# Attention and the last stage in one block: the last attention row carries up products of the last stage's first row

## The reference, cut to what matters

```python
xn  = layernorm(x)
s   = attn(xn)                                   # attention block with its own MLP
g   = silu(ffn(xn))                              # mixture of 8 low-rank maps, gated by a softmax
out = x + s * g

def attn(x):                                     # on xn
    a = rmsnorm(x, ln1_w)
    q, k, v = a @ Wq, a @ Wk * 32**-0.5, a @ Wv  # 16 heads, key width 16, value width 32
    gk = log_sigmoid(a @ Wkg1 @ Wkg2 + bkg2) / 16
    S_t = S_(t-1) * exp(gk_t) + k_t v_t^T ;  o_t = q_t S_t        # linear recurrence over tokens
    o = silu(a @ Wg + bg) * normalize_per_head(o)
    x = x + o @ Wo                               # called xmid in the kernel
    b = rmsnorm(x, ln2_w)
    return x + (silu(b @ W1) * (b @ W3)) @ W2    # W1, W3: 512 x 1408, W2: 1408 x 512
```

## Time and profile before

| | |
|---|---|
| time, median of 3 runs | 1734.0 us (1733.23, 1734.0, 1738.09) |
| the profiled execution | 1738.03 us, of which the profile's span is 1736.3 us |
| granted TensorE clock, mean | 0.979 of full speed |
| TensorE busy | 1640.8 us (95%), 12272 matmuls |
| VectorE, ScalarE, POOL busy | 855.2, 566.9, 153.5 us |
| TensorE in the chain that ended last | 43% of the span |
| HBM | 76.89 MB read, 33.57 MB written |

### The profile page before, as it was taken

One profiled execution on the slowest core, in us unless ns is written; L12 is line 12 of the kernel. 1 busy time (PEld: TensorE's weight loads), 2 busy tenths in 40 slices (PEclk: granted clock), 3 DMA queues, 4 the chain that ended last, 5 costly groups with the idle time before them and its releaser, 6 DMA issues. The chain is left out here.

```text
span 1736.3 us, 30613 instructions
## 1 busy us (share of the span) xinstructions
PE 1640.8 (95%) x12272; PEld 1289.1 (74%) x12272; DVE 855.2 (49%) x1334; ACT 566.9 (33%) x959; POOL 153.5 (9%) x183
## 2 busy tenths in 40 slices
PE   6999999869899999999984899999999999999998
PEld 4777777647677777777763678788787878787886
DVE  5555555237767968877863435141422324141413
ACT  3333333225535635635532241211212121212110
POOL 4650000020101101101000000000000000000000
PEclk9999999989999999999997899999999999999999
DMA  7353332010101101201102324002030303030110
GB/s 159 115 123 75 98 84 73 25 61 2 55 24 54 79 0 79 79 0 79 72 2 97 116 85 173 20 26 94 0 121 0 121 0 121 0 121 0 48 50 25
DMA packets 49429, 110.98 MB, mean 64 GB/s; under 512 B 13088, under 2 KB 24432, under 8 KB 41200
## 3 DMA queue, kind: packets, MB, share of 16 engines
q1 hardware_dynamic: 46640, 97.83, 17.8%
q10 hardware_dynamic: 1152, 8.39, 1.2%
q0 software_dynamic: 1600, 4.25, 0.9%
HBM read 76.89 MB, written 33.57 MB: 64 GB/s over the span
## 5 line engine op out<-in xcount | busy, mean ns | idle before, releaser
L1290 DVE TENSOR_TENSOR m_h<-m_ps,m_silu 128x512 f32<-128x512 f32 x88 | 60.9, 692 | 434.3 <-PE m_ps L1437 434.3
L1363 ACT ACTIVATE m_silu<-m_ps 128x512 f32<-128x512 f32 x88 | 52.5, 597 | 298.8 <-PE m_ps L1437 298.0
L1435 PE MATMUL m_ps<-m_xshi,m_w1hi 128*128 128x512 f32 x352 | 143.3, 407 | 6.3 <-DVE m_xslo L1283 6.3
L1435 PE MATMUL m_ps<-m_xshi,m_w3hi 128*128 128x512 f32 x352 | 140.7, 400 | 4.7 <-ACT m_silu L1363 4.7
L1437 PE MATMUL m_ps<-m_xshi,m_w3lo 128*128 128x512 f32 x352 | 140.0, 398 | 0.0
L1436 PE MATMUL m_ps<-m_xslo,m_w3hi 128*128 128x512 f32 x352 | 140.0, 398 | 0.0
L1436 PE MATMUL m_ps<-m_xslo,m_w1hi 128*128 128x512 f32 x352 | 139.8, 397 | 0.0
L1437 PE MATMUL m_ps<-m_xshi,m_w1lo 128*128 128x512 f32 x352 | 139.7, 397 | 0.0
L892 POOL TENSOR_TENSOR row<-row,a_r 128x512 f32<-128x512 f32 x32 | 48.7, 1553 | 635.6 <-DMA a_r<-scratch_r 635.6
L1435 PEld LDWEIGHTS m_ps<-m_xshi,m_w1hi 128*128 128x128 f32 x352 | 66.5, 189 | 25.2 <-issue 9.5
L831 DVE TENSOR_TENSOR a_a<-a_att,causal 128x1024 f32<-128x1024 f32 x64 | 75.5, 1218 | 16.6 <-PE a_att L1035 16.6
(11 more groups left out here) (245 smaller groups left out, 3834.1 us busy)
## 6 DMA issues: line engine op xcount, KB each, us to landing
row<-scratch_xn SPq DMA_DIRECT2D x16, 1024.0 KB, 5.0
row<-scratch_xmid SPq DMA_DIRECT2D x16, 1024.0 KB, 7.0
m_xt<-in_L_attn_W SPq DMA_DIRECT2D x33, 256.0 KB, 3.2
f_xt<-in_L_attn_x SPq DMA_DIRECT2D x32, 256.0 KB, 8.8
scratch_xn<-row SPq DMA_DIRECT2D x8, 1024.0 KB, 9.7
scratch_gate<-row ACTq DMA_DIRECT2D x8, 1024.0 KB, 3.9
scratch_xmid<-row SPq DMA_DIRECT2D x8, 1024.0 KB, 3.9
row<-scratch_gate SPq DMA_DIRECT2D x8, 1024.0 KB, 10.1
```

The costliest lines, as they stand in the source:

```text
L1290: dve.tensor_tensor(h[n], dense.region(f"b{j}"), silu[n], ALU.mult).then_inc(dense.taken_sem(f"b{j}"), 1)
L1363: act.activation(silu[n], dense.region(f"a{j}"), ACT.Silu).then_inc(dense.taken_sem(f"a{j}"), 1)
L1435: pe.matmul(ps, wh, xh, start=k == 0, stop=False)
```

## The change

Five things are changed together.

1. Attention and last stage share one block. `phase_a` no longer opens a block; it hands its engine streams over as functions, and `phase_m` calls them with a class `Front`. What the last attention row passed over is now work of the last stage's row 0: slot k0 makes up a of block 0, k1 up b of block 0, u and q0 up a and b of block 1, q1 and v1 up a and b of block 2, and z down product 0. Where the next row's x was scaled and split, xmid of row 0 is. The weight pieces 0 to 11 are loaded from the moment VectorE has finished the last product with the q tiles, into `xt`, and 0 to 10 are split between the chunks. The weights now lie per block j (`w[j]`).
2. The squares, the sum on POOL, the mean-square matmul and 1/rms for the last stage move into the attention: in row i they are made of the output of row i - 1, one square in chunk 0, and so on, and 1/rms is stored to HBM (`scratch_r2`, 2 KB a row) and loaded, broadcast, beside x. The buffer of the squares is that of `cum`, so the next row's scan waits for the store. The last row's are made in row 0 of the last stage.
3. In the first stage, row 0 is normed in two halves of two token tiles, W1 comes in four pieces, and ScalarE waits for the bias only after it has filled x.
4. At the end of a row the add of xmid and the multiply by the gate alternate block by block.
5. The last row is turned block by block, and stored in four transfers.

```diff
@@ phase_a: squares of the row before, on ScalarE, POOL, TensorE @@
+            def squares(i, ms):
+                for m in ms:
+                    if m > 1:
+                        act.wait_ge(*count.at("x2sum", i, m - 1))
+                    act.activation(added if m else square, xn[:, m, :], ACT.Square).then_inc(count.sem("x2"), 1)
+            def deviation(i):
+                act.wait_ge(*dense.ready("ms", i))
+                act.activation(added[0:1], dense.region("ms")[0:1], ACT.Ln, bias=eps[0:1]).then_inc(dense.taken_sem("ms"), 1)
+                act.wait_ge(*dense.taken("ms", i))
+                act.activation(added[0:1], added[0:1], ACT.Exp, scale=-0.5).then_inc(count.sem("r2"), 1)
...
+                for m in range(1, KT):
+                    pool.wait_ge(*count.at("x2", i, m + 1))
+                    pool.tensor_tensor(square, square, added, ALU.add).then_inc(count.sem("x2sum"), 1)
...
+                    if c + 1 == NC:
+                        pe.wait_ge(*dense.free("ms", i))
+                        pe.wait_ge(*count.at("x2sum", i))
+                        pe.matmul(dense.region("ms"), avg_all, square, start=True, stop=True).then_inc(dense.ready_sem("ms"), 1)
@@ SP in an attention row, and VectorE ahead of the scans @@
+                sp.wait_ge(*count.at("r2", i))
+                sp.dma_start(row(r2_d, i), added[0:1]).then_inc(count.sem("r2_out"), 16)
+                sp.wait_ge(*count.at("x2", i))
                 sp.wait_ge(*count.at_before("xmid_out", i))
...
+                    dve.wait_ge(*count.at_before("r2_out", i))
                     for gc in range(g * NC, (g + 1) * NC):
@@ phase_m: what fills the last attention row @@
+            def sync(sp):
+                sp.wait_ge(*a.count.at("mqh", NB - 1))
+                sp.wait_ge(*a.dense.ready(f"g{LAST}", NB - 1))
+                sp.dma_start(ln2, ...).then_inc(s_ln2, 16)
+                load_weights(sp, 0, 3 * FRONT + 3)
...
+                # VectorE
+                work = {"split": split, "c0": first_hidden, "u": second_a, "c2": lambda: weights_lo(dve, 6, 7),
+                        "c3": lambda: weights_lo(dve, 7, 9), "upper": second_and_third}
...
+                # TensorE
+                work = {"k0": lambda: up("k0", 0, 0), "k1": lambda: up("k1", 0, 1), "u": lambda: up("u", 1, 0),
+                        "q0": lambda: up("q0", 1, 1), "q1": lambda: up("q1", 2, 0), "z": first_down, "v1": third_b}
@@ SP in row 0 of the last stage @@
+                if first:
+                    sp.wait_ge(*count.at("hlo", 0, FRONT))
+                    sp.wait_ge(*a.count.at("r2_out", NB - 1))
                 ahead("xm")
+                if first:
+                    load_weights(sp, 3 * FRONT + 3, 3 * FRONT + 9)
+                    sp.wait_ge(s_r2, 2)
+                    sp.dma_start(row(a.r2_d, NB), a.v_tok[0:1, 1, :]).then_inc(s_r2_out, 16)
+                    load_weights(sp, 3 * FRONT + 9, len(jobs))
@@ end of a row @@
                 for m in range(KT):
                     dve.wait_ge(*acc.ready(m, i))
                     dve.tensor_tensor(xres[:, m, :], acc.region(m), xres[:, m, :], ALU.add).then_inc(acc.taken_sem(m), 1)
-                for m in range(KT):
                     dve.wait_ge(*acc.taken(m, i))
                     dve.tensor_tensor(gate[:, m, :], xres[:, m, :], gate[:, m, :], ALU.mult).then_inc(count.sem("y"), 1)
```

More of the change, by code:

```diff
@@ new lines, in weights_lo, with up_products @@
+        def weights_lo(dve, first, end):
+            for n in range(first, end):
+                _, hi, lo = jobs[n]
+                dve.wait_ge(s_whi, n + 1)
+                dve.tensor_tensor(lo, stage[n % STAGES], hi.bitcast(F32), ALU.subtract).then_inc(s_wlo, 1)
+        def up_products(pe, ps, i, j, n):
+            pe.wait_ge(s_wlo, 3 * j + n + 1)
+            for k in range(KT):
+                if j == 0 and n == 0:
+                    pe.wait_ge(*count.at("xslo", i, k + 1))
+                wh, wl = w[j][:, n, 0, k, :], w[j][:, n, 1, k, :]
+                xh, xl = (part[:, k, :] for part in xs_hl)
+                pe.matmul(ps, wh, xh, start=k == 0, stop=False)
+                pe.matmul(ps, wh, xl, start=False, stop=False)
+                ins = pe.matmul(ps, wl, xh, start=False, stop=k == LAST)
+            return ins
@@ L1295, in body @@
                 first = isinstance(i, int) and i == 0
-                for j in range(AHEAD, FT):
-                    if first:
+                if first:
+                    weights(FRONT)
+                    dve.wait_ge(*a.count.at("r2_out", NB - 1))
+                for j in range(FRONT if first else AHEAD, FT):
+                    if first and j + 1 < FT:
+                        if j + 1 == FT - 1:
+                            dve.wait_ge(s_r2_out, 16)
                         weights(j + 1)
@@ L1380, in body @@
                 first = isinstance(i, int) and i == 0
-                for j in range(AHEAD, FT):
-                    if first:
+                if first:
+                    weights(FRONT)
+                    act.wait_ge(*a.dense.ready(f"o{LAST}", NB - 1))
+                    act.wait_ge(*a.dense.taken(f"o{LAST}", NB - 1))
+                    last_squares()
+                for j in range(FRONT if first else AHEAD, FT):
+                    if first and j + 1 < FT:
+                        if j + 1 == FT - 1:
+                            act.wait_ge(s_r2_out, 16)
                         weights(j + 1)
@@ L1385, in body @@
                     hi_part(i, j)
-                    if j == FT - 7:
-                        ahead("squares")
-                    if j == FT - 4:
-                        ahead("rms")
+                    if first and j == FRONT + 1:
+                        last_deviation()
                 ahead("hidden")
-            def first_weights(_):
-                weights(0)
-            def second_weights(_):
-                for j in range(1, AHEAD + 1):
-                    weights(j)
-            parts = {"squares": squares, "weights0": first_weights, "rms": rms, "weights": second_weights,
-                     "hidden": first_hidden}
@@ L1480, in body @@
                 ahead("up1b")
-            def before(part):
-                if part == "up0":
-                    pass_over(pe, dense, late, -1)
             def skip(part):
```

510 lines of the change are left out of this document (342 added, 168 removed).

## The result

The changed kernel takes 1685.75 us (median of 4 runs, 1681.19 to 1688.6); the kernel before, measured beside it, 1736.05 (4 runs, 1733.23 to 1742.49). The ratio is 0.9707, with a 95% interval of 0.9689 to 0.9726. The forecast of 1695 and its range of 1686 to 1708 lie above it: the gain is 50 us where 39.4 were worked out.

A forecast was written before the change was run, and what follows sets the result against it. TensorE, busy nearly throughout the 1736.3 us span, was taken as the bound. 39.4 - 0.8 - 1.0 + 2.3 - 1.8 + 1.3 = 39.4 us gained from the median 1734.0 gave 1695 us, range 1686 to 1708.

The forecast's parts named there:

- Rival B: In the rebuilt stretch everything is hidden, even the clock's half rate: gain 47 us, 1687 us; chance 0.12.
- Term 1: Rebuilt stretch, last attention row's first chunk to row 1's first up product: 39.4 us gained, bounds 25 and 48.
- (a): Last attention row: TensorE's first carried product waits for the first weight's low part, made by VectorE: 2.3 us.
- (c): Before the attention's output products: the last carried products must be copied out of the three-bank PSUM ring: 1.2 us.
- (e): Rebuilt stretch: half-rate stretches of TensorE's clock following the waits cost 3.0 us, between 0 and 7.
- Term 2: Mean squares leave seven bodies of the last stage and enter the attention rows: net -0.8 us.
- Term 3: Attention rows: the moved squares, ScalarE steps, POOL adds and 1/rms store cost 0.15 us a row, -1.0 us.
- rival C: The POOL adds block VectorE in each attention row: 2 to 3 us a row, 1715 us; chance 0.07.
- D: Attention's scan waits for the 1/rms store, VectorE late by 6 us in all eight rows: 1736 us; chance 0.03.
- Term 4: The start: bias wait behind the fill, W1 in quarters, norm in halves: +2.3 us, bounds 0 and 3.
- Term 5: Entering attention: 30 more of SP's starting increments stand ahead of the first load: -1.8 us.
- Term 6: The end: output stored in four pieces instead of one transfer: +1.3 us, bounds 0 and 2.

The follow-up runs named there:

- the second run: Changed kernel with 64 unused bytes ahead of w5, so w5 to w10 begin 64 bytes off a multiple of 128: 1694.56 us, 0.9758.
- second ladder: Changed kernel with pads of 224, 32, 32, 160, 32 and 32 bytes ahead of w5 to w10: 1695.83 us in a single execution.
- the first run: Changed kernel with 64 unused bytes ahead of the attention weights and of w0 to w4, which then begin at multiples of 128: 1677.25 us, 0.9656.
- first ladder: Changed kernel with 32 unused bytes ahead of each of w5 to w10: 1692.69 us in a single execution.
- the run with no favourable distance: Changed kernel with pads of 224 bytes ahead of attention's and last stage's x pieces and 32 ahead of w5: 1698.47 us, 0.9778.

## Why the prediction was wrong, step by step

**The step that failed is the unit.** "One 128x512 product costs 0.233 us" was read from rows of one kernel and taken as a property of the instruction. It is one of the instruction and of where its two operands lie. The change moved every tile, 216 of the 396 products of a row went to 0.2267, and v and o of the attention to 0.2291 and 0.2274. With the distances undone the time is 1698.5, inside the range and 3.5 above the forecast; so 12.7 of the 50 us are the addresses', they alone carry the time out of the range, and none of my terms or rivals had them. Rival B, at 1687, comes nearest to the time and was still wrong: the waits were not hidden.

**Term 1** held. Without the addresses the stretch is 140.92 us against 179.11, a gain of 38.2, forecast 39.4. The waits: (a) 2.09, forecast 2.3. (b) 0.95 ahead of the second chunk, forecast 0.5. (c) 2.04, forecast 1.2. (d) nothing in the changed kernel; forecast 2.0. Unforeseen, 3.22 of TensorE's own sequencer. Together 8.3, forecast 6.0. (e) half rate was granted only once in this execution, from 888.6 to 892.0, behind wait (a); nine products took 3.65 us there, 2.10 at full clock, so about 1.5, forecast 3.0. The errors cancel, and partly by luck: twelve profiled executions have the changed kernel's code in this stretch, with 8.1 to 8.6 us of waits, but half rate was granted for 3.4 us in some and for up to 13.6 in others, and the stretch took 139.5 to 143.4. In six of them half rate came with the wait of 3.1 to 3.2 us for the sequencer or just behind it; in the three kernels without that wait it never did. So (e) is between 1.5 and, by an estimate from these rows, some 5 us from one execution to the next.

**Term 2** held in its parts: with the distances undone a row of the last stage is 94.36 us against 95.00, and an attention row 67.96 against 67.10, where the mean square takes 0.86 of TensorE: 0.64 less there, 0.86 more here. With all blocks at 0.2333 (the second run) the row is 94.23, 0.77 less.

**Term 3** was too dear: nothing is left of the 0.15 a row. All 64 masks took 1211 to 1225 ns, the 14 that ran beside GpSimd's adds too, so rival C did not happen; the scan shows no idle time and no DMA ahead of it in the middle row, so neither did D: the store of 1/rms is issued at 714.53 and the scan runs at 718.05. The masks (ns min/median/max):

```profile
L910 DVE TENSOR_TENSOR a_a<-a_att,causal x64: 1211/1216/1225, 409.8 to 917.3; 128x1024 f32<-128x1024 f32 x64
```

**Term 4** held at the first product (3.55, forecast 2.3) and nowhere behind it: undone, it changes the time by less than 1 us. I had priced it as if what comes first also ends first.

**Term 5** held: 1.74, forecast 1.8, shown by the run that moves the increments.

**Term 6** was right for the stores and wrong for the end: 1.3 forecast, -0.7 found from the last down product to the end in the profiled execution, and no time lost by undoing it. The last store is issued 2.7 us before the end instead of 4.6, and at full rate the new end is 1.2 shorter. But I had not asked which banks the transposes write: all wait some 3 us together, half rate mostly follows, and over eleven executions the end is 10.81, as before.

**Missing was** a wait in attention's first row. In the kernel before, ScalarE began on z 2.99 us late there, and TensorE then waited 2.30 and 3.75:

```profile
446.33 0.69 ACT L927 ACTIVATE a_soft<-a_ps,a_bkg 128x512 f32<-128x512 f32 x1 [2.99 <-issue]
...
461.22 0.80 PE L118 MATMUL a_ps<-a_xahi,a_wghi 128*128 128x512 f32 x1 [3.75 <-ACT a_v_tok L936]
```

TensorE was granted half rate from 460.6 to 464.1, where the second of these waits ends. After the change ScalarE begins at once (443.22), TensorE waits 0.79, and the clock stays at full rate there. The distance from the key products carried by attention's first row to those carried by its second is 75.64 us before (75.10 with x and h moved) and 70.0 to 71.9 in the changed kernel and its variants: some 4 us which no term had. What delayed ScalarE is not shown by the trace and was not tried. With the cheaper v and o products (0.5 a row) it is also why attention as a whole got 2 us faster and not 7 slower.

So the sum for the kernel as it was argued (39.4 us) met the run without the addresses (39.2 from span to span) by luck, as its parts show: up to attention's first key product -2.3 (forecast +0.5), attention up to its last row -1.3 (forecast -7.0), the rebuilt stretch 38.2 (39.4), and from there to the end 4.6 (6.5). The missing 4 us in attention make up for the lost start; only terms 1, 2 and 5 were near by themselves.

## What to carry to other kernels

A unit price from a trace holds for the places that its operands had, and an average over a group may have a stop in it: read the single steps. When a change moves the allocation of a kernel that is bound by matmuls, work out each product's distance between the starts of its operands, before and after, and read the price of each distance from whatever block of the trace has it. A stall removed at the start is worth what is left of it at the next fixed meeting of the engines, so read a gain there; and before a step is pulled forward, ask which buffer it writes and who still holds it.

## What the runs showed of the hardware

The time from one 128x512 fp32r matmul to the next, by the start of the moving operand minus that of the stationary one, modulo 256 bytes, at the full granted clock:

| distance | us | where |
|---|---|---|
| 0 | 0.2264 to 0.2283 | the last stage of the kernel before with x and h moved; changed kernel w5 to w10, o; second ladder w6, w10; v and g of the first run without its two longer steps |
| 64 | 0.2286 to 0.2296 | first ladder w10, second ladder w8; changed kernel v; o of the first run; the first stage |
| 32 | 0.2332 to 0.2336 | kernel before, last stage; second ladder w5, w9 |
| 96 | 0.2327 to 0.2336 | kernel before v; first ladder w9 |
| 128, 160 | 0.2322 to 0.2346 | first ladder w8, w7; w0 to w4 of the run with no favourable distance |
| 192, 224 | 0.2328 to 0.2336 | changed kernel w0 to w4; kernel before o; first ladder w5, w6; second ladder w7 |

It is 2.9% of a product. These are paces of products that follow each other without a stop, and an average over a group can hide a stop. The 48 g products of an attention row have distance 0 in the first run and average 0.2311; 45 of their 47 steps have 0.2274, and the two others, 0.30 and 0.335, stand where the last output block begins:

```profile
602.32 0.39 PE L124 MATMUL a_ps<-a_xahi,a_wglo 128*128 128x512 f32 x1
602.62 0.50 PE L122 MATMUL a_ps<-a_xahi,a_wghi 128*128 128x512 f32 x1
602.96 0.40 PE L123 MATMUL a_ps<-a_xalo,a_wghi 128*128 128x512 f32 x1
```

Behind a stop, and behind products at another distance, the low price of distance 0 comes back only after six to ten products: the steps that follow the 0.335 are 0.236, 0.228, 0.233 and 0.231, and only then 0.226 and 0.227. In the first stage, at distance 64 throughout, a group of 24 products that averages 0.2340 has one step of 0.334 behind its first product, and 0.2296 without it. Why the distance matters, and which of the two reads waits, no run shows. The Trainium skill, page "SBUF — State Buffer", section "Who interferes with whom", says that TensorE reads the moving operand and the weights through ports of their own and never waits on anyone; a price that hangs on the distance between these two operands speaks for some dependence between its own two reads, and there the measurement decides.

Profiled executions of the same code differ by 4 us in the rebuilt stretch, by 6.6 us where row 3 of the first stage begins (132.2 to 138.8) and by 1.5 us at the end, so one profile is no measure of a 2 us edit. In the rebuilt stretch and at the end the difference goes with how long half rate was granted behind the waits (3.4 to 13.6 us in the stretch), not with the waits themselves (8.1 to 8.6 us). The row periods behind GpSimd's work repeat within 0.1.
